# A graph kernel's first layer: tile 0's rows and tile 2's sum ahead of the jumps, products and degree sums inside the next tiles' sums

## What is computed

```python
def _layer(x, rows, cols, vals, W, b):            # W0, b0, then W1, b1; vals = 1 / degree
    neigh = segment_sum(vals[:, None] * x[cols], rows, num_segments=N)
    cat = concatenate([x, neigh], axis=1)
    return relu(cat @ W.T + b)

x = layernorm(x + layer(layer(x, W0, b0), W1, b1))      # rows = src, cols = dst
h_sparse = maxk(x @ W_neigh, 32)
neigh = segment_sum(h_sparse[src], dst) / max(deg, 1)
out = layernorm(x + x @ W_self + neigh)
```

## Time and profile before

| | us |
|---|---|
| three timed runs | 674.93, 675.32, 677.57 (median 675.32) |
| the profiled execution | 673.44 |
| its span, first to last instruction | 671.6 |
| TensorE busy, share, mean clock granted | 635.9, 95%, 0.993 |
| VectorE, ScalarE, GpSimd busy | 498.8, 314.5, 110.0 |
| fill stage ends, layer 0's last sum ends | about 187, about 353 |

### The profile page before, as it was taken

The page is one execution under the profiler, slowest core; times in us unless marked ns, Lnnn a source line. Parts: engine busy times, 40 slices in busy tenths (PEclk is TensorE's granted clock), DMA queues, the critical chain, the costliest instruction groups (busy, mean ns, idle before and its releaser), DMA issues.

```text
span 671.6 us, 10824 instructions
## 1 busy us (share of the span) xinstructions
PE 635.9 (95%) x3782; PEld 323.6 (48%) x3783; DVE 498.8 (74%) x1274; ACT 314.5 (47%) x604; POOL 110.0 (16%) x187
## 2 busy tenths in 40 slices
PE   8788899999978999999999899999999999999996
PEld 3466566666533444444444344444444444444442
DVE  7888979999778888888863678787887846633333
ACT  3678799999667766666641222222222210000000
POOL 3001122222111110101000232323223110000000
PEclk9989999999999999999999999999999999999999
DMA  8543644555612222322223999999999933300000
GB/s 215 101 141 110 218 138 159 166 181 162 186 56 58 60 56 56 60 53 65 50 60 95 165 208 174 206 177 186 192 173 187 178 90 116 116 25 26 27 25 23
DMA packets 66741, 79.61 MB, mean 119 GB/s; under 512 B 30320, under 2 KB 59407, under 8 KB 66681
## 3 DMA queue, kind: packets, MB, share of 16 engines
q1 hardware_dynamic: 66681, 78.86, 54.9%
HBM read 38.91 MB, written 33.38 MB: 108 GB/s over the span
## 4 chain that ended last, share of the span: by engine, by line
PE 66%; DVE 15%; DMA 9%; ACT 4%; issue 3%; POOL 2%; SPq 1%; DVEq 0%; POOLq 0%; ACTq 0%
PE pair L1550 23%; PE bank L1648 10%; PE pair L1648 10%; PE bank L1474 6%; DMA tr_sb<-part 5%; PE bank L1445 4%; PE pair L1365 4%; PE bank L1453 3%; PE pair L1453 3%; DMA own_in<-own_dram 2%; DVE m L953 2%; DVE hots L648 2%; DVE work L958 2%; POOL part L556 1%; DVE tree L831 1%
## 5 line engine op out<-in xcount | busy, mean ns | idle before, releaser
L1550 PE MATMUL pair<-xs,ct 125*128 125x512 f16 x625 | 139.4, 379 | 2.3 <-issue 2.3
L1550 PE MATMUL pair<-a,ct 125*128 125x512 f16 x625 | 138.9, 379 | 0.0
L648 DVE TENSOR_TENSOR hots<-iota,jobs 125x1792 f16<-125x1792 f16 (+1 forms) x100 | 103.6, 1069 | 3.4 <-PE pair L1365 2.9
L1550 PEld LDWEIGHTS pair<-xs,ct 125*128 125x128 f16 x625 | 61.7, 99 | 75.0 <-issue 2.8
L1550 PEld LDWEIGHTS pair<-a,ct 125*128 125x128 f16 x625 | 62.0, 99 | 73.8
L1079 ACT ACTIVATE slab<-pair 125x875 f16<-125x875 f32 (+1 forms) x100 | 83.3, 854 | 11.3 <-PE pair L1365 6.8
L1231 ACT ACTIVATE a<-ct 125x1000 f16<-125x1000 f16 (+1 forms) x75 | 80.4, 1072 | 9.7 <-DMA c_dram<-slab 8.1
L538 POOL TENSOR_TENSOR own_in<-own_in,bias_sb 125x256 f32<-125x256 f32 x50 | 37.8, 757 | 246.5 <-DMA own_in<-own_dram 246.5
L1648 PE MATMUL bank<-xs,ct 125*128 125x512 f16 (+1 forms) x325 | 71.5, 379 | 0.0
L1648 PE MATMUL pair<-xs,ct 125*128 125x512 f16 x300 | 66.2, 379 | 0.0
L1299 ACT ACTIVATE sd<-mv,epsb 125x1 f32<-125x1 f32 x25 | 7.4, 294 | 113.9 <-DVE mv L1015 113.9
(11 more groups left out here) (202 smaller groups left out, 758.4 us busy)
## 6 DMA issues: line engine op xcount, KB each, us to landing
c_dram<-slab SPq DMA_DIRECT2D x25, 683.6 KB
ct<-c_dram SPq DMA_DIRECT2D x25, 683.6 KB
own_in<-own_dram SPq DMA_DIRECT2D x50, 125.0 KB
own_dram<-own SPq DMA_DIRECT2D x25, 125.0 KB
own_dram<-own_st SPq DMA_DIRECT2D x25, 125.0 KB
x_in<-in_x_dram SPq DMA_DIRECT2D x25, 125.0 KB
z_dram<-z_st SPq DMA_DIRECT2D x25, 125.0 KB
a<-z_dram SPq DMA_DIRECT2D x5, 625.0 KB
```

Source lines behind the costliest of these rows:

```text
L648: v.tensor_tensor(hots[k][:, :, :, :].rearrange("p w g (a d) -> p (w g) a d", d=2), iota, job, ALU.is_equal).then_inc(win_hot, 1)
L1550: ins = mm(agg[k % 3][0:lhs.shape[1], :], lhs, parts[l][:, t, :], start=t == 0, stop=t == NT - 1, skip_group_check=True)
```

## The change

- The weights' halves are stored in steps 4 and 5, each by its own wait; ScalarE waits for both ahead of the last set of step 8, not the first.
- `layer_start` sums all 25 blocks of tile 2. `layer_begin` takes the place of `first_trees`: behind the two trees it has the inverse, both halves and the low part of tile 0. Only then come the jumps.
- ScalarE's `h_high(0)` stands right behind its jump, ahead of all `degree` sums.
- Layer 0's loops: product T-2 and a degree sum stand between the blocks of tile T's sum, by two tables of block numbers; from tile 10 on the tile's own degrees are summed at block 22, from tile 11 on product T-2 opens the sum. VectorE's tree for T+1 comes in iteration T, its first sum ahead of the low part. `own1_out`, `store_own1` and `a1_low` are one tile later, ahead of T's own rows.

```diff
@@ constants
+LATE_MM = {4: 14, 5: 12, 6: 10, 7: 8, 8: 6, 9: 4, 10: 2}
+LATE_DEG = {4: 12, 5: 10, 6: 8, 7: 5, 8: 3, 9: 0}
+DEG_AT = 22
@@ SyncE
                 store_slab(t)
-                if t == HELD - 2:
-                    sp.wait_ge(w_split, 4)
-                    for l in range(2):
-                        sp.dma_start(wparts_dram[l], w_parts[l][:, :, :, :].rearrange("p h q f -> p (h q f)")
-                                     ).then_inc(w_stored, 16)
+                if 3 < t < 6:
+                    sp.wait_ge(w_split, 2 * t - 6)
+                    sp.dma_start(wparts_dram[t - 4], w_parts[t - 4][:, :, :, :].rearrange("p h q f -> p (h q f)")
+                                 ).then_inc(w_stored, 16)
...
             for T in range(NT):
                 if T + 2 < NT:
                     load_own(0, T + 2)
+                if T > 1:
+                    store_own1(T - 2)
                 turn(T)
-                if T:
-                    store_own1(T - 1)
+            store_own1(NT - 2)
@@ VectorE
-            def sum_tree(T):
+            def sum_tree(T, first=0, end=9):
...
-                step(v.tensor_tensor(tree[:, :], quint[0], quint[1], ALU.add))
+                if first == 0:
+                    v.tensor_tensor(tree[:, :], quint[0], quint[1], ALU.add).then_inc(tree_step, 1)
+                count[0] += 1
+                if end == 1:
+                    return
+                dve.wait_ge(tree_step, count[0])
...
-            def first_trees():
+            def low_half(T):
+                dve.wait_ge(hi_ready, T + 1)
+                v.scalar_tensor_tensor(part[T % 2][0:P, F:2 * F], t2[T % 2][:, :], 0.0, part[T % 2][0:P, 0:F],
+                                       ALU.max, ALU.subtract).then_inc(lo_ready, 1)
+
+            def layer_begin():
                 for free in tr_free:
                     dve.wait_ge(free, 2 * NT + 1)
                 sum_tree(0)
                 sum_tree(1)
+                invert(0)
+                dve.wait_ge(dve_step, first_half(0, 0))
+                second_half(0, 0)
+                low_half(0)
...
-                first_trees()
+                layer_begin()
...
-            invert(0)
             for T in range(NT):
-                dve.wait_ge(dve_step, first_half(0, T))
-                second_half(0, T)
-                dve.wait_ge(hi_ready, T + 1)
-                v.scalar_tensor_tensor(part[T % 2][0:P, F:2 * F], t2[T % 2][:, :], 0.0, part[T % 2][0:P, 0:F],
-                                       ALU.max, ALU.subtract).then_inc(lo_ready, 1)
+                if T > 1:
+                    a1_low(T - 2)
+                if T:
+                    dve.wait_ge(dve_step, first_half(0, T))
+                    second_half(0, T)
+                    if T < NT - 1:
+                        sum_tree(T + 1, 0, 1)
+                    low_half(T)
+                    if T < NT - 1:
+                        sum_tree(T + 1, 1, 9)
                 if T + 1 < NT:
                     invert(T + 1)
-                if T + 2 < NT:
-                    sum_tree(T + 2)
-                if T:
-                    a1_low(T - 1)
+            a1_low(NT - 2)
             a1_low(NT - 1)
@@ ScalarE
                 for t in range(1, NT):
-                    if t == HELD:
-                        act.wait_ge(w_stored, 32)
                     own = OWN[t]
                     quick_copy(t, 0)
...
+                    if t == HELD:
+                        act.wait_ge(w_stored, 32)
                     quick_copy(t, 3)
...
+            act.wait_ge(part_zeroed, 2)
+            h_high(0)
             act.wait_ge(slab_stored[0], BOTH * 13)
...
                 if T + 1 < NT:
                     degree(T + 1, 0)
-                if T == 0:
-                    act.wait_ge(part_zeroed, 2)
-                    h_high(0)
                 if T + 1 < NT:
                     degree(T + 1, 1)
                     degree(T + 1, 2)
+                if T > 1:
+                    own1_out(T - 2)
                 if T:
                     h_high(T)
...
-                if T:
-                    own1_out(T - 1)
+            own1_out(NT - 2)
             own1_out(NT - 1)
@@ TensorE
                 degrees(1)
-                aggregate(0, 2, 0, 9)
+                aggregate(0, 2, 0, NT)
...
-            aggregate(0, 2, 9, 20)
+            product(0)
+            aggregate(0, 3, 0, 14)
             degrees(2)
-            aggregate(0, 2, 20, NT)
-            product(0)
-            aggregate(0, 3, 0, 8)
+            aggregate(0, 3, 14, 16)
             product(1)
-            aggregate(0, 3, 8, 17)
-            degrees(3)
-            aggregate(0, 3, 17, NT)
-            product(2)
-            degrees(4)
+            aggregate(0, 3, 16, NT)
             for T in range(4, NT):
-                aggregate(0, T, 0, NT)
-                if T + 1 < NT:
-                    degrees(T + 1)
-                product(T - 1)
-
+                for b in range(NT):
+                    if b == LATE_DEG.get(T):
+                        degrees(T - 1)
+                    if b == LATE_MM.get(T, 0):
+                        product(T - 2)
+                    if b == DEG_AT and T + 1 not in LATE_DEG:
+                        degrees(T)
+                    aggregate(0, T, b, b + 1)
+            product(NT - 2)
```

More of the change, by code:

```diff
@@ L838, in sum_tree, with invert, first_half, second_half @@
                 v.tensor_tensor(deg16[T % 2][:, 1, :], tree2[:, 0:PC], deg16[T % 2][:, 0, :], ALU.subtract).then_inc(deg_split, 1)
-            def first_trees():
+            def invert(T):
+                dve.wait_ge(deg_done, T + 1)
+                step(v.tensor_scalar(rdeg[0][:, T:T + 1], bank[7][0:P, T:T + 1], 1.0, None, ALU.max))
+                step(v.reciprocal(rdeg[0][:, T:T + 1], rdeg[0][:, T:T + 1]))
+                v.tensor_scalar(rdeg[1][:, T:T + 1], rdeg[0][:, T:T + 1], scales[0:P, NSC + 7:NSC + 8], None, ALU.mult
+                                ).then_inc(deg_ready, 1)
+            def first_half(l, T):
+                k = l * NT + T
+                dve.wait_ge(own_biased, k + 1)
+                dve.wait_ge(deg_ready, T + 1)
+                dve.wait_ge(agg_done, k + 1)
+                return noted(v.scalar_tensor_tensor(t2[k % 2][:, :], agg[k % 3][0:P, 0:F], rdeg[l][:, T:T + 1],
+                                                      own_in[k % 2][:, :], ALU.mult, ALU.add))
+            def second_half(l, T):
+                k = l * NT + T
+                v.scalar_tensor_tensor(t2[k % 2][:, :], agg[k % 3][0:P, F:2 * F], rdeg[l][:, T:T + 1], t2[k % 2][:, :],
+                                       ALU.mult, ALU.add).then_inc(t2_ready, 1)
+            def low_half(T):
[3 more added lines that the diff above has]
+            def layer_begin():
                 for free in tr_free:
@@ L844, in first_trees @@
                 sum_tree(1)
+                invert(0)
+                dve.wait_ge(dve_step, first_half(0, 0))
+                second_half(0, 0)
+                low_half(0)
+            ahead = done[0]
             dve.wait_ge(matched_ready, 1)
@@ L877, in _ @@
                     tr_copy(NT - 1, g)
-                first_trees()
+                layer_begin()
+            done[0] = ahead
             with dve.If(total < E):
@@ L896, in _ @@
                             v.tensor_copy(xstage[:, :], xs32[:, ds(t - 1, 1), :].rearrange("p o f -> p (o f)")).then_inc(own_staged, 1)
[L897 to L913, removed]
-            def second_half(l, T):
-                k = l * NT + T
-                v.scalar_tensor_tensor(t2[k % 2][:, :], agg[k % 3][0:P, F:2 * F], rdeg[l][:, T:T + 1], t2[k % 2][:, :],
-                                       ALU.mult, ALU.add).then_inc(t2_ready, 1)
+                layer_begin()
             def a1_low(T):
```

## The result

The changed kernel takes **681.22 us** (median of 10 runs, 679.11 to 684.31); the kernel before, beside it on the same chip, 675.37 (10 runs, 674.93 to 677.74). The ratio is 1.0079 with a 95% interval of 1.0057 to 1.0101: slower by 0.8%. The prediction, 671.4 us and faster, has the wrong sign, and its range (to 674.2) does not hold the time.

A forecast was written before the change was run, and what follows sets the result against it. The prediction took TensorE, busy 95% of the span, to bound the kernel. Its terms, -2.7 - 2.2 + 0.6 + 0.4 = -3.9 us, gave a forecast of 671.4 us, range 669.2 to 674.2.

The forecast's parts named there:

- The weights' store: Fill stage, step 8: ScalarE's wait for the store of the split weights goes whole, 2.7 us gained.
- The start of layer 0: Tiles 0 to 5: TensorE's gaps of 6.4 become 2.5 plus a new wait of 1.9; 2.2 us gained.
- TensorE's jump stays: Start of layer 0: behind tile 2's 25 blocks the jump still costs TensorE 2.33 us before product 0.
- The cadence: Layer 0's ramp and steady tiles: VectorE's loop of 6.05 to 6.53 us decides; 0.6 us lost.
- From tile 10 on 6.78 is allowed and both bounds fit: Layer 0's steady tiles: VectorE's loop of 6.05 to 6.53 fits within TensorE's 6.78 us a tile; no loss.
- Rival 2: Layer 0, SyncE: own rows' store delays transposes; slower if they land at 4.9 us, 681 us at 5.1; chance 0.06.
- Rival 1: Layer 0's ramp: VectorE's loop meets GpSimd's bias add every tile; 2.0 us lost, not 0.6; 673.4 us; chance 0.34.
- Matmuls within sums: Layer 0, TensorE: products and degree sums between another tile's blocks cost what they cost outside; nothing lost.
- The end of layer 0: The last degree sum brings VectorE later to the last first half, lengthening layer 1's first product wait; 0.4 us lost.
- all is handed on: From layer 1 on: nothing changed, TensorE bounds it with small transpose waits, so earlier gains and losses carry through.

The follow-up runs named there:

- the mended kernel: The changed kernel with SyncE's store ahead of the load and ScalarE's column sums one tile later; 667.79 us, ratio 0.9877.
- TensorE's part alone: The kernel before with tile 2's sum whole (25 blocks, not 9) ahead of TensorE's jump, nothing else; 674.89 us, ratio 0.9983.

## Why the prediction was wrong, point by point

The terms were -2.7, -2.2, +0.6 and +0.4; between the marks they measured -2.6, 0.0, +7.5 and -0.1, and layer 1 added 1.0.

- **The weights' store: right.** 2.7 forecast, 2.6 between the marks, in the kernel with that part alone too; the timed gain of that kernel is 4.0 (2.8 to 5.4).
- **The start of layer 0: the sum of the waits was right, its parts and the outcome were not.** 2.33 + 1.9 was forecast, 0.39 + 3.81 measured, 4.2 both ways. The degree sum came where the arithmetic of the nine column sums put it: 204.6 forecast, 203.59 on a clock that ran 1.16 us earlier (tile 0's degree sum at 185.74, not 186.90), so 204.75. The failed step is "TensorE's jump stays": with 25 blocks ahead of it, all but 0.39 us is hidden, and the kernel with tile 2's sum alone has no such gap either. TensorE thus came 1.9 us sooner to the degree sum and stood there 1.9 longer. With 0.16 more for each gap, as the prediction counted them, 6.4 became 4.5: 1.9 gained. And then the clock fell behind that wait, which no term had, and took 1.7 of it: 0.0 by the end of tile 5's sum, within 0.2.
- **The cadence: the step that gave the wrong sign.** "From tile 10 on 6.78 is allowed and both bounds fit" looked at VectorE's loop alone, as if the only thing it could wait for were its own work. I had put down that `own1_out`, `store_own1` and `a1_low` move, and priced the hop through TensorE's degree matmuls, but not the wait that `a1_low` brings ahead of the first half: through ScalarE's copy, the one buffer, the store, and SyncE's load ahead of it, back to VectorE's own second half. That loop takes 7.0 us on average. +0.6 was forecast, +7.5 came. Of that, 6.5 goes when the store is put ahead of the load and 5.7 when the buffer is doubled; the steady tiles are back at 6.78 and 6.82.
- **Rival 2 named the place and the time (681 us), not the mechanism.** The store does stand ahead of the transpose, and the transposes land in 4.3 us, not 2.9; that is still inside the 4.4 us that I had given them, and below the 4.9 from which they were to decide. With two buffers they stay late and the loss is gone. Its chance of 0.06 was for a cause that was worth 1.3 us; that its time came out is luck.
- **Rival 1: its mechanism exists, and the 0.6 for the ramp was somewhat small.** In the mended kernel the add falls on the tree's last step in most tiles (median 631 ns, 224 alone). VectorE's loop, forecast between 6.05 and 6.53, shows there as 6.42 a tile from degree sum to degree sum, and the ramp pays about 1 us, less than the rival's 2.0. From tile 10 on it does no harm. In the changed kernel the slower ring covers it.
- **Matmuls within sums: right, nothing.** In the mended kernel a turn of the ramp in which nothing waits takes the 6.35 us of its parts with the product inside the sum (248.54 to 254.89), and a steady tile, with the degree sum inside, 6.78 as before the change.
- **The end of layer 0: forecast +0.4, measured -0.1.** From layer 1's first block to its first product it is 19.96 before, 19.90 after and 20.00 in the mended kernel, which has no ring. The later correction does not show there; why was not looked into.
- **Layer 1: "all is handed on"** missed 1.0 us: the clock fell at layer 1's first product. Whether that belongs to the change stays open (below).

## What to carry to other kernels

When work is moved between tiles, follow each buffer that exists once: which DMA frees it, what stands ahead of that DMA in its queue, and what that in turn waits for. If the way leads back to the engine that waits for the buffer's writer, it is a ring, and its length, not the busy time of any engine, sets the pace; here one swap of two calls on SyncE was worth 6.7 us. Work ahead of a jump pays only if what feeds the next wait is brought forward as well: TensorE's part alone left layer 0 at 167.3 us; with tile 0's rows ahead of VectorE's jump and ScalarE's column sums out of the way the start gained 4.8 us.

## What the runs showed of the hardware

- **A jump of TensorE can be hidden.** With nine blocks ahead of it, it left a gap of 2.33 us (1.48 in the kernel with the weights' part alone; why these differ is open); with 25 blocks 0.39, 0.27 and 0.41 in three kernels. In the five others with 25 blocks a wait of 0.45 to 0.77 us for a transpose or a degree sum stands in that place, so no more than that can be left of the jump. VectorE, with one step of 0.43 us right ahead of its jump, stood 3.41 behind it in the changed kernel and, with one of 0.23, 2.71 before.
- **An idle TensorE pays twice.** Behind a wait of 3.81 us the granted clock was 0.52, and 1.7 us were lost; with matmuls in the wait the product and the 21 blocks behind it were back at 1.46 and 4.70 us.
- **The length of the wait alone doesn't tell.** At layer 1's first product the clock fell in four profiles (the changed kernel and three experiments) behind waits of 2.22 to 2.35 us, and did not in five others behind 2.12, 2.24, 2.30, 2.39 and 2.73. What decides is open; none of the runs was made to tell.
- **A store of 125 KB took 4.0 to 4.5 us** when a load and a transpose went out beside it, and the transpose behind the two took 4.3 to 4.4 and not 3.0. The DMA packets of the stretch from 230 to 340 us took 34.9% of the 16 engines' time, those before 25.8%, for nearly the same bytes (6.15 and 6.20 MB).
